# Preactivated convolution and token attention, images by image: the layout of images on the partitions and the convolution rebuilt

## The reference

```python
x = x + L0(_gn(x))                      # _gn: each image and channel to mean 0, variance 1
# L0:
y = conv(x, conv_w, padding=15, rhs_dilation=5)   # 32 channels -> 1, 7 x 7 taps, 5 apart
imp = sigmoid(gelu(bn(y)))              # one importance map per image
xs = x * imp
idx = sort(top_k(imp.reshape(B, -1), 192))
tokens = xs at idx (192 x 32 per image) + make_pos[idx]
t2 = attention (8 heads of 4), layernorm, feed-forward, layernorm of tokens
xf = x normalised, with the 192 pixels at idx replaced by t2
```

## Time and profile before

| what | value |
|---|---|
| timed runs (3) | 1163.17, 1157.36, 1159.79 us; median 1159.79 |
| span of the profiled execution | 1225.6 us, mean granted clock 0.884 |
| PE busy | 971.3 us, 79%; weight loads 762.4 |
| DVE / ACT / POOL busy | 835.0 (68%) / 774.3 (63%) / 631.8 us (52%) |
| DMA | 247.82 MB, 202 GB/s over the span |
| chain that ended last | PE 38%, DVE 20%, ACT 12%, issue 9%, DMA 9%, unknown queue 6%, POOL 5% |

### The profile page before, as it was taken

How to read it: one execution, slowest core, us unless ns; L and a number is a source line. 1 busy time by engine, 2 the same in 40 slices (tenths; PEclk the granted TensorE clock), 3 DMA queues, 4 the chain that set the end, 5 groups by cost and what they waited for, 6 DMA issues and landing times.

```text
span 1225.6 us, 21628 instructions
## 1 busy us (share of the span) xinstructions
PE 971.3 (79%) x6440; PEld 762.4 (62%) x6440; DVE 835.0 (68%) x2114; ACT 774.3 (63%) x1899; POOL 631.8 (52%) x851
## 2 busy tenths in 40 slices
PE   3986865689888988898889889986786786488676
PEld 2765643577667766776678667865664565366544
DVE  5345776488558967896879677976694676455644
ACT  2545644486547786877688768875866575267543
POOL 4333316632665368546854576557516655562352
PEclk8998988799879999999899999998987589699855
DMA  9998977555566989898989888965453555436778
GB/s 244 314 264 227 272 210 180 146 159 157 133 156 184 266 217 237 236 291 208 233 238 274 228 238 227 265 187 143 132 169 98 132 154 151 123 98 195 212 221 269
DMA packets 176252, 247.82 MB, mean 202 GB/s; under 512 B 65512, under 2 KB 71912, under 8 KB 176136
## 3 DMA queue, kind: packets, MB, share of 16 engines
q1 hardware_dynamic: 167944, 244.03, 71.9%
q0 software_dynamic: 8192, 2.40, 1.5%
HBM read 124.53 MB, written 121.80 MB: 201 GB/s over the span
## 4 chain that ended last, share of the span: by engine, by line
PE 38%; DVE 20%; ACT 12%; issue 9%; DMA 9%; another core or an unknown queue 6%; POOL 5%; SPq 1%; ACTq 0%; DVEq 0%; POOLq 0%
PE cv L527 10%; PE sc L646 7%; PE pp L659 4%; PE xb L511 4%; PE tr L561 3%; DVE res L1350 3%; ACT wgt L843 3%; PE ib L574 2%; ACT pr L872 2%; PE ms L675 2%; DMA table<-xt 2%; DMA X<-in_x 2%; DVE stats L1126 2%; DMA tok_pos<-in_pos,idx 2%
## 5 line engine op out<-in xcount | busy, mean ns | idle before, releaser
L527 PE MATMUL cv<-X,w_conv 128*128 128x330 f32 (+1 forms) x1024 | 302.2, 422 | 11.6 <-issue 5.9
L527 PEld LDWEIGHTS cv<-X,w_conv 128*128 128x128 f32 x1024 | 193.3, 203 | 45.9 <-issue 12.1
L843 ACT ACTIVATE wgt<-ib,eps_col,mom 128x440 f32<-128x440 f32 (+1 forms) x256 | 177.6, 701 | 46.3 <-DVE res L1350 22.0
L1145 DVE TENSOR_SCALAR_CACHE_REDUCE junk<-flat,th 128x379 bf16<-128x379 f32 x200 | 120.6, 603 | 115.3 <-ACT th L829 89.3
L511 PE MATMUL xb<-cst,X 128*110 128x128 f32 x900 | 153.7, 297 | 48.8 <-ACT xt L809 28.3
L646 PE MATMUL sc<-k_b,qm 128*128 128x192 f32 x768 | 172.2, 353 | 16.2 <-DVE pixf L1245 7.3
L1046 POOL TENSOR_SCALAR res<-res,mom 128x440 f32<-128x440 f32 (+1 forms) x152 | 96.0, 634 | 171.0 <-DVE res L1350 169.3
L1350 DVE SCALAR_TENSOR_TENSOR res<-tr,mom,wgt 128x440 f32<-128x440 f32 (+1 forms) x192 | 122.2, 641 | 71.4 <-PE tr L561 31.0
L809 ACT COPY xt<-xb 110x512 f32<-110x512 f32 x225 | 131.6, 585 | 58.9 <-PE xb L511 30.7
L872 ACT ACTIVATE pr<-sc,least 128x192 f32<-128x192 f32 x384 | 137.1, 415 | 31.0 <-DVE least L1314 18.6
L659 PE MATMUL pp<-cst,pr 128*96 128x128 f32 x768 | 122.5, 284 | 33.6 <-ACT pt L883 25.4
(11 more groups left out here) (170 smaller groups left out, 1534.2 us busy)
## 6 DMA issues: line engine op xcount, KB each, us to landing
table<-xt SPq DMA_DIRECT2D x240, 224.0 KB
rt<-table SPq DMA_DIRECT2D x240, 224.0 KB
...
conv_rows<-cvr SPq DMA_DIRECT2D x64, 188.0 KB
y<-conv_rows SPq DMA_DIRECT2D x64, 165.4 KB
...
```

The source lines that it names most:

```text
L527: last = mm(cv[:, 0:CUT[half]], w_conv[:, 4 * q + z], X[:, m % XI, at0:at0 + CUT[half]], start=z == 0, stop=z == 3)
L843: last = A(wgt[:, n % 2, at0:at0 + w], ib[:, at0:at0 + w], ACT.Identity, scale=mom[:, NB * g + b, 2:3], bias=eps_col[:, 1:2])
```

## The change

**Layout.** A group is now two pairs of images. Partition 2 (32 b + c) + s of `X` holds channel c of image b of the pair, and of its 22 row blocks of 5 those of parity s: 11 blocks, 55 tiles, no padding. `X` has 3 pair buffers (before 4 of one image). A pair has V = 14 units, the last of 3 tiles; U = 28, 110 tiles a group. A unit never holds two pairs, so the split by image goes, except where the ring `res` wraps. ACT's copy from the transposed tile to `xt` reorders the columns from (image, channel, parity) to (parity, image, channel), so that a table row is again 32 channels, and on the way back a tile's partitions are parity, image, channel.

**Moments.** bn_stats runs over all 128 partitions in 12 pieces of 504 columns, one a slot; `average` (PE) averages mean and variance of the two parities with one 2-column matmul into `ib`, DVE makes the pair's moments of it (`moments`, five small operations), POOL computes rstd, and `average_turn` (PE) brings mean and rstd into the other partition order, again through `ib`. The quadrant copies on ACT and POOL go. `spread` waits for the last reader of `ib` of either kind.

**Convolution.** Now X stands in the array and the taps move: for each row residue r (0 to 4) of a pair, 11 matmuls, one for each block q, write 14 rows (2 images x 7 column taps) of 5, 7 or 8 results into `cv`, accumulating over the blocks. The result has the image's column on the partitions. ACT copies it into `zs` (every fifth place), and after the fifth residue `conv_last` sums the seven taps with 7 matmuls per image, whose moving operand is a shifted identity. ACT copies the map to `yy`. `conv_rows`, `y7`, `round_out`, `taps_in` and `importance_sum` go.

**Order.** POOL normalises a fifth at a time (rows of one residue, strided), all after the pair's last transpose. The table of slots is new:

```diff
-        LOAD, INTO, MOMENTS, NORMAL = -21, -11, -5, (-2, -1, -1)
-        TAPS, SUM = (10, 17, 25, 31), (15, 20, 28, 32)
-        GELU, IMP_OUT, FLAT, SEARCH, IMP_IN = 33, 35, 38, 40, 58
+        LOAD, INTO, STATS, AVERAGE, TURN, NORMAL = -28, -15, -16, -4, 1, (-2, -1, 1, 3, 5)
+        LAST, GELU, IMP_OUT, FLAT, SEARCH, IMP_IN = 10, 26, 28, 31, 33, 51
...
-        SCATTER, BACK, IMPB = 122, 127, (123, 127, 135, 142)
+        SCATTER, BACK, IMPB = 115, 120, (116, 120, 128, 134)
...
-                for z in range(first, last_z):
-                    blk_in = 2 * q + z
-                    pe.wait_ge(xn_ok, upto(xn_ok, g, 3 * b + blk_in // 2))
-                    at0 = BW * blk_in + CUT[0] * half
-                    last = mm(cv[:, 0:CUT[half]], w_conv[:, 4 * q + z],
-                              X[:, m % XI, at0:at0 + CUT[half]], start=z == 0, stop=z == 3)
+                bank = cv[0:H, 0:2 * ZC].rearrange("p (a t) -> p a t", t=TB)
+                for q in range(6, BLKS) if late else range(6):
+                    lo, hi = max(0, 2 * q - 3), min(TB, 2 * q + 5)
+                    at0 = H * (5 * q + r)
+                    last = mm(bank[:, :, lo:hi], X[:, m % XI, at0:at0 + H], w_conv[:, :, lo + 3 - 2 * q:hi + 3 - 2 * q],
+                              start=q == 0, stop=q == BLKS - 1, skip_group_check=True)
...
+            def conv_last(g, h, b):
...
+                for k in range(KS):
+                    last = mm(cv[0:H, H * b:H * b + H], zs[:, b, k, :], shift[:, 5 * k:5 * k + H], start=k == 0, stop=k == KS - 1)
...
+            def average(g, h):
...
+                ib_read.append((avg_rd, upto(avg_rd, g, h)))
+                mm(ib[:, MOM:MOM + 2], pair_avg, own_mom[:], start=True, stop=True).then_inc(avg_ok, 1)
...
+            def average_turn(g, h):
...
+                ib_read.append((turn_rd, upto(turn_rd, g, h)))
+                mm(ib[:, MOM:MOM + 2], halves_apart, mom[:, PAIRS * g + h, 1:3], start=True, stop=True).then_inc(turn_ok, 1)
...
-                nc.scalar.copy(xt[0:H, n % 4, :], bank[0:H, :]).then_inc(xt_cp, 1)
+                w = 128 * tiles(u)[1]
+                nc.scalar.copy(xt[0:H, n % 4, 0:w].rearrange("p (a s c) -> p a s c", s=2, c=2 * C),
+                               bank[0:H, 0:w].rearrange("p (a c s) -> p a s c", s=2, c=2 * C)).then_inc(xt_cp, 1)
...
+                if r < 5:
+                    nc.scalar.copy(zs[:].rearrange("p b k (t r) -> p (b k) t r", r=5)[:, :, :, r],
+                                   cv[0:H, 0:2 * ZC].rearrange("p (a t) -> p a t", t=TB)).then_inc(cv_cp, 1)
...
-            CHUNKS = (0, 460, 918, 1376, 1834, 2292, 2750, 3026, 3300)
...
+                lo, hi = 504 * n, 504 * n + (506 if n == 11 else 504)
...
+            def moments(g, h):
+                m = PAIRS * g + h
+                dve.wait_ge(avg_ok, upto(avg_ok, g, h))
+                post(v.tensor_tensor(mom[:, m, 0:1], own_mom[:, 0:1], ib[:, MOM:MOM + 1], ALU.subtract))
+                post(v.tensor_copy(mom[:, m, 1:2], ib[:, MOM:MOM + 1]))
```

567 lines of the change are left out of this document (268 added, 299 removed).

## The result

| | before | changed |
|---|---|---|
| median of the timed runs | 1159.39 us (6 runs, 1157.36 to 1164.01) | 1149.14 us (6 runs, 1148.74 to 1152.32) |
| ratio, 95% interval | | 0.9909, 0.9881 to 0.9936 |
| forecast | | 1085 us, 1040 to 1150 |

The changed kernel is faster by 0.9%, where 6.4% were forecast. The time lies at the upper edge of the range; what failed is the size of the gain.

The account below looks back on a forecast made before the run. TensorE, VectorE and ScalarE were taken to bound the full stretch together through handovers, DMA bytes the start. Stretches over 361 slots summed to 1147 of 1225.6 us, ratio 0.936, carried to the timed median as 1085 us, range 1040 to 1150.

Parts of the forecast that it names:

- The start: First transpose to first count, bound by DMA bytes: 446 KB a slot at 269 GB/s, 84 us for 101.
- A tap record: Convolution's tap matmuls on TensorE: 95 ns taken per record, convolution 210 us in all, 27 us less.
- the rival of strided reads: ScalarE's strided copies (xt read, zs written) cost double per element, 117 us more; total 1151 us; chance 0.09.
- strided matmul writes: Rival: tap matmuls writing PSUM in 14 runs of 8 columns stream at half pace; 1227 us; chance 0.05.
- Statistics: VectorE's bn_stats: 192 calls of 504 columns at 671 ns, 11 us less in all.
- The spread's waits for the handovers: Spread waits until VectorE has read the moments from bank ib: 15 times 1.0 us, +15 us, ends 0 and 25.
- full stretch: First spread to last input transpose, all stages on: 89 slots, 115.8 us a group, 383 us with new waits, for 427.
- The sum: Adding the stretches over 361 slots instead of 380: 1147 of 1225.6 us, ratio 0.936, carried to 1085 us.
- search stretch: First count to first spread: 86 slots at 3.20 us instead of 3.25, 275 us for 280.
- the tail: Last count to last spread: 89 slots at 2.38 us, 212 us for 219.
- a group period still at 125: Named sign of a wrong forecast: time per group in the full stretch staying near the old 125.5 us.
- lumps: Rival: uneven work per slot eats the gain, group period stays 125.5 us; 1123 us; chance 0.17.

Follow-up runs that it names:

- bytes_back: Changed kernel plus one extra DMA copy per unit to unused memory, 32.5 MB in all; ratio to before 1.0104.
- before, again: The kernel before, unchanged, profiled a second time; span 1165.0 us where the first profile had 1225.6, timed ratio 1.0002.
- zs_plain: Changed kernel with ScalarE's copies of the convolution residues to zs written contiguously, so the map's rows stand in another order; ratio to before 0.9906.
- turn_first: Changed kernel with VectorE's pair moments and the copy for average_turn placed ahead of the two layernorms in their slot; ratio to before 0.9905.

## Why the prediction was wrong

**Right.** The start: 84.1 us, forecast 84, and it goes with DMA time, as bytes_back shows. Its terms met by luck, though: a slot moved some 494 KB (282 GB/s x 1.75 us), not 446, and at 282 GB/s, not 269. DMA 214.9 MB, forecast 215. A tap record starts every 97 ns ((1.32 - 0.16)/12), forecast 95. Copies to xt with every second element read: 578 ns for all shapes, 585 in the earlier trace rows and forecast, so neither the rival of strided reads nor the one of strided matmul writes came true. The Trainium skill (Advanced Engine Details and Errata, PSUM Cachelines) warns that non-contiguous patterns in PSUM slow matmuls significantly; in this trace neither the matmuls into 14 runs of 5, 7 or 8 floats nor ScalarE's read at every second float cost anything that shows. The shift matmuls, which write 110 contiguous columns, start no faster: 14 records of L498 from 501.87 us on cover 1.52 us, (1.52 - 0.16)/14 = 97 ns each. Statistics 675 ns, forecast 671. Busy times: TensorE 912 (some 920), VectorE 766 (750), ScalarE 734.5 (715); TensorE's would be 898 from the second profile of before.

The time of one rival, ScalarE's strided copies at double price, was 1151 us and is the nearest to the 1149 measured. That is luck as well: the large term of it, the copies to xt, cost nothing, and the small one is worth 1 us.

**A size.** ScalarE's excess is the copy to zs, every fifth place written: 722 ns, where the earlier trace rows and the slope gave 412 and the contiguous write takes 419 (changed, then zs_plain):

```profile
L809 ACT COPY zs<-cv 110x308 f32<-110x308 f32 x80 | 57.7, 722 | 23.6 <-PE cv L488 23.4
```

```profile
L809 ACT COPY zs<-cv 110x308 f32<-110x308 f32 x80 | 33.5, 419 | 22.8 <-PE cv L488 22.6
```

24 us of ScalarE, worth 1 us (its total fell by 17). The spread's waits for the handovers were forecast at 15 us and are 15.6 in the full stretch (5.8 and 9.8), though 9.8 of them in three places of 3.3 us; taking them away was worth 6 us.

**The step that failed** is the one under "The sum": busy time per group less the savings, idle time scaled by 28/30, the mean of three engines as the period. It did two things that the runs contradict.

First, it took work removed as time removed. In the full stretch it took 6.1, 11 and 7.5 us off the three engines' busy time per group, 8.2 in the mean, and all of it off the period. Less than that went: against before, again, TensorE's busy time per group fell from 107.7 to 104.3 us, VectorE's from 101.2 to 94.7, ScalarE's from 95.6 to 92.0, 4.5 in the mean (of ScalarE's missing 3.9, 3.0 are the copies to zs). That alone is 12 of the 28.6 us by which the sum from the second profile missed the stretch; the other 17 are idle time, which in the mean of the engines grew from 16.1 to 24.9 us a group, where the sum had it at 19.7 with the handovers. And what did go was worth little: at the measured worth of relief, between 0.18 and 0.40 for TensorE, 0.08 for VectorE and nearly nothing for ScalarE, it is 1.3 to 2.0 us a group instead of 8.2. Over the 3.18 groups this is an estimate of 20 to 22 us. It is a rough one, since the worth hangs on the place: VectorE's 0.08 is that of its sum, and of its second layernorm more came back than was taken.

Second, it let time and idle time shrink with the number of slots. In the search stretch that held (86 slots in both, 269.1 and 270.9 us), and nearly so up to the last count (3.67 us a slot, then 3.73). In the tail it did not: there the convolution plays no part, a slot went from 2.27 to 2.43 us, while a group takes 68 us in both kernels (206.7 for 91/30 groups, 216.2 for 89/28), and the changed kernel has more groups of it to go. The sum had scaled it per slot, 200 instead of 216. In the full stretch neither a slot (3.92, then 4.36 us) nor a group (117.6, then 121.9) kept its time. Behind the first count the kernel before takes 1044.4 us for 325 slots, the changed one 1042.5 for 309: the same time, 3.21 a slot against 3.37, where the sum said 3.19. In groups it is 10.83 of 96.4 us against 11.04 of 94.5: a group got 2.0% cheaper, while the way through the pipeline, counted in groups, got 1.9% longer. Search steps, gathers and score rounds need their slots whatever the image layout is.

**What would have shown it beforehand.** The prediction named a group period still at 125 as the sign of its failure. With the second profile of before it is 121.9 after 117.6. The rival "lumps" came closest in its mechanism: it said that the period stays and the gain of work is eaten. Its time, 1123, was still too low, since it scaled the tail by slots as well.

**Open.** Of the full stretch's 28.6 us some 10 to 12 are not accounted for: relief takes 20 to 22, the idle time that didn't shrink 3, and the handovers were counted at 15 and gave only 9. No run gives the changed kernel 30 slots a group or the one before 28, so the denser slots, with the same attention work in fewer of them, stand as an untested cause, beside the DMA time of the full stretch. What makes VectorE's second layernorm so dear in both kernels is shown as a fact and not taken apart. No order tried beats the changed kernel by more than the measurement tells: turn_first, at 0.9905, is its equal.
